# Scores of a group in two bursts instead of four, on one Trainium2 core

## What is computed

```
q = layernorm(x) @ Wq.T + bq;  k = ctx @ Wk.T + bk;  v = ctx @ Wv.T + bv
scores = q k / sqrt(16), masked;  w = softmax(scores);  x = x + tanh(g0) * ((w v) @ Wo.T + bo)
h = layernorm(x);  x = x + tanh(g1) * ((silu(h @ fp8(gate) * gs) * (h @ fp8(up) * us)) @ fp8(down) * ds)
```

## Time and profile before

| | |
|---|---|
| runs | 712.65, 713.08, 716.04 us |
| profiled execution, span from first to last instruction | 711.1 us |
| busy PE / DVE / ACT / POOL | 614.3 / 513.0 / 369.2 / 236.9 us |
| iteration starts (first maxima burst) r = 0, 1, 2, 5, 6, 7 | 71.06, 131.69, 203.55, 440.39, 515.18, 579.37 us |

### The profile page before, as it was taken

One profiled execution on the slowest core, in us unless ns is written; L12 is line 12 of the kernel. 1 busy time (PEld: TensorE's weight loads), 2 busy tenths in 40 slices (PEclk: granted clock), 3 DMA queues, 4 the chain that ended last, 5 costly groups with the idle time before them and its releaser, 6 DMA issues. The chain is left out here.

```text
span 711.1 us, 15863 instructions
## 1 busy us (share of the span) xinstructions
PE 614.3 (86%) x5133; PEld 351.0 (49%) x5133; DVE 513.0 (72%) x1543; ACT 369.2 (52%) x672; POOL 236.9 (33%) x321
## 2 busy tenths in 40 slices
PE   4737568777898999899958999899999998999997
PEld 3624223422465546554635546554665455457583
DVE  3436887796789787987749887987799798564321
ACT  3434474443565646565435745565466466556251
POOL 2101010110243423452232533452245344337374
PEclk9856775758799999999989999999999999999999
DMA  7494940730171014501261014601260100110000
GB/s 253 180 206 162 229 135 16 142 40 2 45 151 34 2 60 125 66 10 46 62 131 24 3 54 122 76 10 46 66 81 2 46 32 19 36 40 18 11 21 30
DMA packets 52862, 50.37 MB, mean 71 GB/s; under 512 B 6478, under 2 KB 40363, under 8 KB 52779
## 3 DMA queue, kind: packets, MB, share of 16 engines
q1 hardware_dynamic: 52778, 49.32, 29.1%
HBM read 35.15 MB, written 9.44 MB: 63 GB/s over the span
## 5 line engine op out<-in xcount | busy, mean ns | idle before, releaser
L786 DVE CUSTOM_DVE_ANT_0 junk<-sc,mq 128x256 bf16<-128x256 f32 x512 | 185.2, 420 | 49.1 <-PE sc L868 47.7
L795 DVE SCALAR_TENSOR_TENSOR ws<-sc,padc,mask_k 128x1024 f32<-128x1024 f32 x128 | 163.6, 1280 | 56.1 <-issue 35.1
L613 ACT ACTIVATE ws<-ws 128x1024 f32<-128x1024 f32 x128 | 135.2, 1057 | 46.4 <-DVE ws L795 45.0
L483 POOL TENSOR_TENSOR ff<-ga,up 128x256 f32<-128x256 f32 x96 | 69.8, 727 | 169.8 <-DVE ga L756 161.9
L603 ACT ACTIVATE up<-work,fuse_s 128x256 f32<-128x256 f32 x96 | 45.4, 472 | 105.8 <-PE work L993 105.5
L993 PE MATMUL work<-h_h,wg 128*128 128x256 f16 x384 | 92.0, 279 | 9.0 <-DVE cl L706 8.8
L893 PE MATMUL av<-ws,va 128*32 128x256 f32 x1024 | 90.7, 430 | 4.4 <-issue 4.4
L993 PE MATMUL work<-h_l,wg 128*128 128x256 f16 x384 | 91.7, 278 | 0.0
L993 PE MATMUL work<-h_h,wu 128*128 128x256 f16 x384 | 91.4, 277 | 0.0
L993 PE MATMUL work<-h_l,wu 128*128 128x256 f16 x384 | 91.2, 277 | 0.0
L868 PE MATMUL sc<-ks,qs 48*128 48x256 f16 x512 | 55.0, 299 | 22.1 <-DVE ws L795 9.5
(11 more groups left out here) (122 smaller groups left out, 1034.0 us busy)
## 6 DMA issues: line engine op xcount, KB each, us to landing
qs<-q_scratch SPq DMA_DIRECT2D x48, 128.0 KB, 6.2
cin<-in_ctx SPq DMA_DIRECT2D x8, 512.0 KB, 4.7
xin<-in_x SPq DMA_DIRECT2D x8, 512.0 KB, 6.2
xb<-in_x SPq DMA_DIRECT2D x8, 512.0 KB, 3.6
att_u<-un SPq DMA_DIRECT2D x128, 32.0 KB, 2.2
out_x<-yt SPq DMA_DIRECT2D x16, 256.0 KB, 2.0
ks<-k_scratch SPq DMA_DIRECT2D x48, 64.0 KB, 4.8
q_scratch<-qh SPq DMA_DIRECT2D x8, 256.0 KB, 2.4
```

The source lines that it names most:

```text
L483: pool.tensor_tensor(ff[:, n % RING, :], ga[:, n % RING, :], up[:, n % RING, :], ALU.mult).then_inc(ff_done, 1)
L613: act.activation(ws[:, unit, :, :], ws[:, unit, :, :], ACT.Exp, scale=1.0 / SSC).then_inc(exp_done, 1)
L786: last = dve.tensor_tensor_reduce(junk[:, HPG * t + j, :], sc[k][:, place(j)], mq[p_][:, t, :], 1.0, -3.4e38, ALU.add, ALU.max, mx[:, t, c ...
L795: dve.scalar_tensor_tensor(out=ws[:, 2 * (u % 2) + kt, :, :], in0=sc[kt][:, :].rearrange("p (j l) -> p j l", j=HPG), scalar=padc[par][:, k ...
```

## The change

The four bursts of a group are issued in two steps instead of four: at k = 0 maxima t = 0 and sum scores kt = 0, at k = 2 maxima t = 1 and sum scores kt = 1. Maxima always use `sc[0]` and sum scores always `sc[1]`. Both halves of the weighted sum of the previous group follow the burst at k = 2. DVE's reads and ACT's exponentials move with them. The waits of `maxima` and `scores` become "all earlier maxima read" and "all earlier sum scores read". The pieces stay at their steps.

```diff
-SUMS_AT = (1, 2)
+SUMS_AT = (2, 2)
@@ m_unit
-            if k > 1:
+            if k % 2:
                 return None
             off, g = (0, 5 + u) if u < 3 else (1, u - 3)
-            return (off, g, k) if there(r, off) else None
+            return (off, g, k // 2) if there(r, off) else None
@@ ACT, after the pieces of the step
-                    if step % 4 > 1 and there(r, 0):
-                        n = 16 * r + 2 * u + step % 4 - 1
-                        act.wait_ge(t_free, n)
-                        unit = 2 * (u % 2) + step % 4 - 2
+                    if step % 2 == 0 and there(r, 0):
+                        kt = step % 4 // 2
+                        act.wait_ge(t_free, 16 * r + 2 * u + kt + 1)
+                        unit = 2 * (u % 2) + kt
@@ DVE
-                            last = dve.tensor_tensor_reduce(junk[:, HPG * t + j, :], sc[k][:, place(j)],
+                            last = dve.tensor_tensor_reduce(junk[:, HPG * t + j, :], sc[0][:, place(j)],
...
-                    if k > 1 and there(r, 0):
-                        kt = k - 2
+                    if k % 2 == 0 and there(r, 0):
+                        kt = k // 2
...
-in0=sc[kt][:, :].rearrange("p (j l) -> p j l", j=HPG),
+in0=sc[1][:, :].rearrange("p (j l) -> p j l", j=HPG),
@@ PE, maxima
-                past(pe, m_free, 16 * b + 2 * g - 1 + t)
-                past(pe, t_free, 16 * (b - 1) + 2 * (g + 2) + t + 1 if g < 6 else 16 * b + 2 * (g - 6) + t + 1)
+                past(pe, m_free, 16 * b + 2 * g + t)
@@ PE, scores
-                past(pe, t_free, 16 * b + 2 * g + kt - 1)
-                done = 16 * b + 2 * (g + 5) + kt + 1
-                past(pe, m_free, min(done, 16 * NB) if isinstance(done, int) else done)
+                past(pe, t_free, 16 * b + 2 * g + kt)
@@ PE, steps
-                    if k > 1 and there(r, 0):
-                        scores(r, u, k - 2, par)
-                    if k in SUMS_AT and u == 0 and there(r, -1):
-                        weighted(r - 1, 7, SUMS_AT.index(k), 1 - par)
-                    if k in SUMS_AT and u > 0 and there(r, 0):
-                        weighted(r, u - 1, SUMS_AT.index(k), par)
+                    if k % 2 == 0 and there(r, 0):
+                        scores(r, u, k // 2, par)
+                    for kt in range(TT):
+                        if k == SUMS_AT[kt] and u == 0 and there(r, -1):
+                            weighted(r - 1, 7, kt, 1 - par)
+                        if k == SUMS_AT[kt] and u > 0 and there(r, 0):
+                            weighted(r, u - 1, kt, par)
```

More of the change, by code:

```diff
@@ L795, in steps @@
                         dve.scalar_tensor_tensor(
-                            out=ws[:, 2 * (u % 2) + kt, :, :], in0=sc[kt][:, :].rearrange("p (j l) -> p j l", j=HPG),
+                            out=ws[:, 2 * (u % 2) + kt, :, :], in0=sc[1][:, :].rearrange("p (j l) -> p j l", j=HPG),
                             scalar=padc[par][:, kt:kt + 1], in1=mask_k[:, kt:kt + 1, :].broadcast_to([P, HPG, L]),
@@ L855, in work_bank, with maxima @@
                 return work[BANK[piece]]
-            def maxima(b, g, t, p_, k):
+            def maxima(b, g, t, p_):
                 if g == 0 and t == 0:
@@ L863, in maxima @@
                         pe.wait_ge(set_free, len(SETUP))
-                past(pe, m_free, 16 * b + 2 * g - 1 + t)
-                past(pe, t_free, 16 * (b - 1) + 2 * (g + 2) + t + 1 if g < 6 else 16 * b + 2 * (g - 6) + t + 1)
+                past(pe, m_free, 16 * b + 2 * g + t)
                 for j in range(HPG):
                     pair, at = 2 * g + j // 2, 64 * (j % 2)
-                    last = mm(sc[k][:, place(j)], qs[p_][at:at + 3 * HD, pair, t * P:(t + 1) * P],
+                    last = mm(sc[0][:, place(j)], qs[p_][at:at + 3 * HD, pair, t * P:(t + 1) * P],
                               ks[p_][at:at + 3 * HD, g, :], start=True, stop=True)
@@ L875, in scores @@
                     pe.wait_ge(mr_in, 64 * (2 * b + g // 4 + 1))
-                past(pe, t_free, 16 * b + 2 * g + kt - 1)
-                done = 16 * b + 2 * (g + 5) + kt + 1
-                past(pe, m_free, min(done, 16 * NB) if isinstance(done, int) else done)
+                past(pe, t_free, 16 * b + 2 * g + kt)
                 for j in range(HPG):
                     pair, at = 2 * g + j // 2, 64 * (j % 2)
-                    last = mm(sc[kt][:, place(j)], ks[p_][at:at + 3 * HD + 2, g, kt * P:(kt + 1) * P],
+                    last = mm(sc[1][:, place(j)], ks[p_][at:at + 3 * HD + 2, g, kt * P:(kt + 1) * P],
                               qs[p_][at:at + 3 * HD + 2, pair, :], start=True, stop=True)
@@ L1017, in steps @@
                         off, g, t = unit
-                        maxima(r + off, g, t, par if off == 0 else 1 - par, k)
-                    if k > 1 and there(r, 0):
-                        scores(r, u, k - 2, par)
-                    if k in SUMS_AT and u == 0 and there(r, -1):
-                        weighted(r - 1, 7, SUMS_AT.index(k), 1 - par)
-                    if k in SUMS_AT and u > 0 and there(r, 0):
-                        weighted(r, u - 1, SUMS_AT.index(k), par)
+                        maxima(r + off, g, t, par if off == 0 else 1 - par)
+                    if k % 2 == 0 and there(r, 0):
[5 more added lines that the diff above has]
+                            weighted(r, u - 1, kt, par)
                     for name, n, b, odd in pieces(r, par, step):
```

## The result

The changed kernel takes 723.0 us (median of four runs, 719.9 to 724.5) against 713.8 us for the kernel before on the same chip: 1.012 times as long, 95% interval 1.009 to 1.015. It is slower by 9.2 us; the forecast was 714.0 with a range of 705 to 721. The profiled execution spans 721.2 us against 711.1.

A forecast was written before the change was run, and what follows sets the result against it. PE was taken to set the pace in iterations 2 to 5, DVE close. 711.1 - 5.6 - 1.5 - 0.9 + 2.5 + 6 = 711.6, with 2.0 from span to median 713.6, given as 714, range 705 to 721.

The forecast's parts named there:

- Part 1: Fewer array shape changes on PE, 0.10 us each: saves 3.2 a full iteration, 2.2 in iteration 6, 1.3 in 7.
- Part 2: Pieces behind two DVE reads: steps 4 to 7 lose 1.3, other places 0.2; full iterations net -1.4 each, four -5.6.
- less to do behind it, which gives back some: Steps 4 to 7, iterations 2 to 5: one add less on DVE cuts 1.6 us late to 1.3, bounds 0.8 and 2.5.
- Part 4: Idle times at steps 4 to 7 drop PE's clock and slow `gu`: +6 us over iterations 2 to 5, between 0 and 10.
- six tenths: Share taken of the 10 us clock loss over four iterations, between none and the three quarters seen before: +6.
- Before, little hung on it, since DVE was behind anyway: Step 7, kernel before: the half-clock `gu` after an idle time was taken to cost little.
- Part 3: The start: maxima through one bank pair delay iteration 0 about 5 us, iterations 0 and 1 return 2.5: +2.5, bounds -1 and +6.
- iteration 0 starts about 5 late: Iteration -1: six burst periods of about 2.1 instead of 1.38 us cost 4.3, and q 0 comes behind another burst.
- levelling costs only a third: Iterations 6 and 7: DVE lag where both engines are level takes a third, leaving -1.5 and -0.9 us.
- done in time but at step 14: Full iterations: the add two steps earlier, awaited by the sum scores burst, is in time except at step 14.
- Slower, one mechanism: Rival: both idle times at steps 4 to 7 drop the clock (+10), the start keeps 5: 720 us; 0.3 for over 716.7.
- The bursts do drain: Rival: maxima and sum scores bursts drain between them, losing 1.6 of 3.2 saved per full iteration: 721 us; chance 0.05.

The follow-up runs named there:

- h1_loop: The kernel before with the whole change in iterations 2 to 5 only, the old order elsewhere: 712.93 us, 0.9975 times the kernel before.
- e3_mid: The changed kernel, but DVE does its pieces of the step before between the maxima's reductions and the add of the masks: 725.76 us, 1.0185 times the kernel before.
- e5_halves: The kernel before with only both halves of the weighted sum at k = 2, the four bursts staying at their steps: 708.47 us, 0.992 times the kernel before.
- e2_start: The changed kernel, but in iteration -1 the maxima keep their old steps and both bank pairs: 717.45 us, 1.0047 times the kernel before.
- e4_sums12: The changed kernel with the weighted halves back at k = 1 and 2, so the bursts alone: 736.26 us, 1.029 times the kernel before.

## Why the prediction was wrong

The profiled execution took 721.2 us where the sum had 711.6, 9.6 more. 5.3 of them come from iterations 6 and 7 (forecast -2.4, measured +2.9), 4.2 from what lies before iteration 2 (+2.5, measured +6.7) and 0.2 from iterations 2 to 5.

**Part 1, changes of shape: right.** PE's busy time in iteration 5 fell by 3.5 us for a predicted 3.2, and the burst pair has 0.23 between its starts for 0.22. The Trainium skill (TensorEngine Tiling (Array Packing), Key Properties) has the drain at a change of mode and none between tiles of one mode, and these rows agree, maxima and sum scores with their 48 and 50 rows being one mode.

**Part 2, iterations 2 to 5: the sum right, its terms not.** Predicted -5.6 and +6 for the clock, +0.4; measured +0.6, and `h1_loop` shows the same flatness in the time. But iteration 5, where no `gu` was slow in either kernel, gained 0.2 and not 1.4. The step that fails is "less to do behind it, which gives back some": I took 1.3 for steps 4 to 7, but PE's waits for `ga` and `cl` grew by 1.9 + 0.3 = 2.2, and the group is 1.8 longer although changes of shape are saved in it too. Where `ga` and `cl` stand behind one read, in `e3_mid`, the same four steps last 10.29 us. Another 1.5 of waiting came where I had 0.2: 0.8 at the sum scores and 0.7 at x2T. That DVE was close to PE (62.94 of 74.59) is not by itself the reason. `e5_halves` takes 1.3 us off PE in the same iteration (69.67 busy) with DVE as busy (62.41), and 0.95 of it shows in the time. The largest loss is where a bank stands behind two reads.

**Part 4, the clock: the place right, the size too large.** The windows of the `gu` of steps 5 and 7 in the changed kernel, one per line from iteration 2 to 5 (busy PE and PEld, granted clock), answer to the earlier trace rows:

```profile
222.43:225.56 3.13, 3.13 (x16) 2.19 (x15) 0.51 0.25 50
229.85:231.49 1.64, 1.64 (x16) 1.47 (x16) 1.00 0.05 10
298.59:300.23 1.64, 1.64 (x16) 1.47 (x15) 1.00 0.28 55
304.53:307.54 3.01, 3.01 (x15) 2.11 (x16) 0.53 0.00 0
382.19:385.10 2.91, 2.91 (x15) 2.12 (x15) 0.55 0.21 43
389.75:392.82 3.07, 3.07 (x16) 2.14 (x16) 0.52 0.02 5
459.93:461.56 1.63, 1.63 (x15) 1.46 (x15) 1.00 0.24 50
465.86:467.49 1.63, 1.63 (x15) 1.46 (x16) 1.00 0.00 0
```

Four of eight idle times were followed by half clock (1.2 GHz), near the six tenths taken. But before, three of the four `gu` of step 7 were slow already, and after, only two of them: in iterations 2 and 4 the one at step 5 is slow (and in iteration 4 both), in iteration 3 only the one at step 7. Over the eight, what exceeds the 1.64 us of a fast one (from the first start of the 16 to the last) is 1.49 + 1.37 + 1.27 + 1.43 = 5.6 us after and 1.03 + 1.47 + 1.51 = 4.0 before, with 0.5 more after at the `gu` of step 1 in iteration 4, which is slow in both. So the clock added some 2 us and not 6, and without it iterations 2 to 5 changed by -1.4, or by four times the -0.2 of iteration 5, and not by -5.6. Two errors of over 4 us cancelled: that the sum of these iterations came out is luck.

The step that fails here is "Before, little hung on it, since DVE was behind anyway". Steps 4 to 7 of the kernel before last 10.08 us in iteration 5, without a slow `gu`, and 11.56 in iteration 3, with one that takes 1.47 too long: it was paid in full before, too. After it is the same (11.90 and 13.29, for 1.37). And `e2_start`, whose loop is that of the changed kernel, has the slow one in iteration 5 and none in iteration 3: its steps 4 to 7 last 13.34 and 11.91. I had priced the slow `gu` of the changed kernel on top of ones that cost nothing before, though three of them were already there and only one was added.

**Part 3, the start: here the prediction failed.** I wrote "iteration 0 starts about 5 late"; it starts 9.4 late. 1.8 of these are not the change's: the first maxima burst of all, ahead of which no instruction differs, starts at 49.23 against 47.44, and in the kernels here that keep the old start it starts anywhere between 46.7 and 49.9. The change's share is 7.6. The mechanism and its 5 hold from xT to q 0: 54.00 to 67.69 is 13.7 us, before 52.18 to 60.91, 8.7. The term that is missing is 2.6 behind q 0: the first burst of iteration 0 waits 2.89 us at 80.44 for the reductions of its forerunner, since DVE stands at its part of q 1 first:

```profile
78.13 0.88 DVE L700 SCALAR_TENSOR_TENSOR ql<-work,bq_c,qh 128x256 f16<-128x256 f32 x2 [2.46 <-ACT qh L573]
78.92 0.41 DVE L786 CUSTOM_DVE_ANT_0 junk<-sc,mq 128x256 bf16<-128x256 f32 x1
```

I stopped the count of periods at step 26, although the same bank pair serves steps 28, 30 and 0. What iterations 0 and 1 gave back, 2.6 for 2.5, is right by luck. Steps 16 to 19 of iteration 1, where I had most of it, last 12.32 us (granted clock 0.66) against 12.42 (0.86); in `e2_start` they last 9.45 (0.95), so what there is to gain there shows only where the clock holds. The gain of the changed kernel lies in steps 4 to 7 of iteration 0 (7.23 against 10.71), where PE waits 3.2 us for the load of `cin` before and, coming there later, does not after. So iteration 2 starts 6.7 late for a predicted 2.5.

**Iterations 6 and 7: the wrong sign.** Predicted -1.5 and -0.9, measured +2.5 and +0.4. That levelling costs only a third there was an argument by analogy: without cT there is no borrowed bank, and I had no other wait in view. The added wait that I listed, the sum scores for the add of two steps before, I called "done in time but at step 14" for the full iterations, and for 6 and 7 I did not look. PE's waits in iterations 6 and 7 of the changed kernel (522.55 to 649.24):

```profile
PE sc L878 <- DVE ws L795: 4.4, 8, 0.8
PE sc L867 <- DVE mx L786: 3.0, 2, 1.5
PE work L976 <- ACT x2n L564: 0.9, 1, 0.9
PE av L950 <- DVE mx L786: 0.6, 1, 0.6
```

These are 8.9 us against 4.7 before, and the add was late eight times. With 4.2 more of waiting and 1.1 for two `gu` partly at half clock, against 2.2 saved where I had 3.5 (PE's busy time fell by 1.1 in spite of those `gu`), the two iterations should be 3.1 longer, and are 2.9. That these waits come from the single bank pairs is read from the rows, and no run tests it. The times of `h1_loop` and `e2_start` together show only that about 4 us are lost outside iterations -1 and 2 to 5; the lengths put them into iterations 6 and 7. Why the changes of shape saved 2.2 there and not 3.5 stays open.

**The rivals.** "Slower, one mechanism" gave 720 through ten us of clock and a start of 5. The time lies near it, but by another way: little clock, more start, and an end that loses. "The bursts do drain" fell with the 0.23. My doubt, 0.33 for slower, was on the right side for partly wrong reasons.

## What to carry to other kernels

When two readers of a buffer pair are put behind one another, count the time from the write to the last read for every pass over that pair, up to the first use after the stretch changes, and do it for the stretches with another mix (start and end) as carefully as for the loop. Where two engines are this close (PE busy 95%, DVE 84% of iteration 5), work taken off the first is not time won until the waits between them have been recounted: of the 3.5 us saved here, 0.2 were won, and of the 1.3 saved by `e5_halves`, which puts no read behind another, 0.95. And before a change of two parts is judged, each part should be run alone: here one was worth -6 us and the other +22.

## What the runs showed of the hardware

A burst into a single bank pair costs at half clock 2.31 us a period (four reductions and the way there and back), against 1.38 with two pairs, where DVE's reductions alone set the pace.

An idle time of PE of 2.2 to 2.5 us was followed by half clock in about half the cases, in steps whose instructions are the same in every iteration: in the changed kernel after cT 1 in iterations 2 and 4 and not in 3 and 5. Which of them it hits differs from execution to execution of the same loop (after the idle time at step 7 iterations 3 and 4 in the changed kernel, iteration 5 alone in `e2_start`) and how many from kernel to kernel (`e3_mid` has one slow `gu` in iterations 2 to 5, `e4_sums12` eight). In both kernels each slow one among steps 4 to 7 lengthened these four steps by what it took too long (1.0 to 1.5 us) or up to 0.2 more. This makes up several us of the difference between kernels with the same waits. The Trainium skill (TensorE: Matmul & The Clock Gate, Loop structure matters more than you think) ties the clock to how dense the loop's matmuls are. The rows agree in kind; that the same step with the same idle time goes either way, they show beyond it.
